# A fused feed-forward / attention / feed-forward block: picked rows corrected in DRAM, and one bias addition moved from GpSimd to VectorE

## The reference, cut to what matters

```python
x = x + 0.5 * ffn(layernorm(x), gate_w, gate_b, w1, w2)          # x: 8 x 1024 x 512
x = x + attn(layernorm(x), Wq, bq, Wk, bk, Wv, bv, Wo, bo)
x = x + 0.5 * ffn(layernorm(x), gate_w, gate_b, w1, w2)

def ffn(x):                                    # 32 experts, each picks 8 tokens of every batch
    probs = softmax(x @ gate_w.T + gate_b, axis=tokens)
    vals, idx = top_k(probs, 8)                # per batch and expert, over the 1024 tokens
    merged = sum_k vals * x[idx]               # one vector per batch and expert
    o = w2(gelu(w1(merged)))                   # both with a bias row, hidden size 2048
    return zeros.at[idx].add(vals * o)         # only picked tokens change

def attn(x):                                   # 16 heads of 32, linear attention
    q, k, v = exp(x Wq + bq), exp(x Wk + bk), x Wv + bv
    return (q . cumsum(k v^T)) / (q . cumsum(k)) @ Wo + bo
```

## Time and profile before

| | us |
|---|---|
| median of 3 runs (2296.61 to 2299.26) | 2297.79 |
| the profiled execution | 2299.73 |
| its span, first to last instruction | 2298.0 |
| TensorE busy | 1981.2 (86%) |
| TensorE weight loads busy | 1172.0 (51%) |
| ScalarE busy | 815.3 (35%) |
| VectorE busy | 734.2 (32%) |
| GpSimd busy | 647.2 (28%) |
| granted TensorE clock, mean | 0.937 |
| DMA | 762.76 MB, 332 GB/s over the span |

### The profile page before, as it was taken

The page is one execution under the profiler, slowest core; times in us unless marked ns, Lnnn a source line. Parts: engine busy times, 40 slices in busy tenths (PEclk is TensorE's granted clock), DMA queues, the critical chain, the costliest instruction groups (busy, mean ns, idle before and its releaser), DMA issues.

```text
span 2298.0 us, 44195 instructions
## 1 busy us (share of the span) xinstructions
PE 1981.2 (86%) x18664; PEld 1172.0 (51%) x18664; DVE 734.2 (32%) x1248; ACT 815.3 (35%) x1525; POOL 647.2 (28%) x783
## 2 busy tenths in 40 slices
PE   5789999999999999999999999999775666656666
PEld 3546666666666666676767767766521111111111
DVE  6731111111111111467677677677410000000011
ACT  6831121111111122477777777777510000000000
POOL 7620000000000000377777777777402000000002
PEclk9899999999999999999999999999987768887788
DMA  9999999999999999366554454444699999999997
GB/s 361 346 392 401 422 428 420 422 423 419 430 418 427 420 420 397 120 221 217 158 161 149 151 161 155 151 142 157 233 412 424 427 389 428 428 427 428 428 428 335
DMA packets 113844, 762.76 MB, mean 332 GB/s; under 512 B 21736, under 2 KB 21864, under 8 KB 76016
## 3 DMA queue, kind: packets, MB, share of 16 engines
q1 hardware_dynamic: 101552, 701.35, 76.9%
q10 hardware_dynamic: 9216, 50.34, 5.3%
q0 software_dynamic: 2880, 8.25, 0.9%
HBM read 648.65 MB, written 106.43 MB: 329 GB/s over the span
## 4 chain that ended last, share of the span: by engine, by line
PE 57%; DMA 23%; POOL 8%; ACT 5%; issue 4%; SPq 1%; DVE 1%; POOLq 0%; ACTq 0%; DVEq 0%
PE ps L316 53%; DMA big<-in_L_ffn_w 22%; PE ps L320 3%; POOL big L1475 2%; POOL s L1478 2%; DMA last_scratch<-idx 1%; SPq L18 1%; POOL big L1449 1%; ACT big L600 1%; POOL s L1460 1%; ACT big L1301 1%; POOL big L1480 1%; PE ps L787 1%; ACT big L585 1%; POOL big L1472 1%
## 5 line engine op out<-in xcount | busy, mean ns | idle before, releaser
L316 PE MATMUL ps<-big 128*32 128x512 f32 (+4 forms) x13792 | 985.2, 418 | 225.7 <-DMA big<-in_L_ffn_w 183.9
L316 PEld LDWEIGHTS ps<-big 128*32 128x32 f32 (+2 forms) x13792 | 385.9, 127 | 720.3 <-issue 383.4
L324 DVE TENSOR_TENSOR big<-ps,big 128x128 f32<-128x128 f32 (+3 forms) x375 | 343.7, 931 | 676.3 <-PE ps L787 509.6
L316 PE MATMUL ps<-wth,xth 128*128 128x512 f32 x768 | 311.8, 406 | 1.5 <-DVE xtl L324 1.5
L316 PE MATMUL ps<-wtl,xth 128*128 128x512 f32 x768 | 299.6, 390 | 0.0
L316 PE MATMUL ps<-wth,xtl 128*128 128x512 f32 x768 | 299.3, 390 | 0.0
L835 ACT COPY big<-ps 128x512 f32<-128x512 f32 x64 | 37.5, 586 | 650.8 <-PE ps L316 650.8
L1467 POOL TENSOR_SCALAR big<-big 128x1 f32<-128x1 f32 x64 | 12.3, 192 | 847.3 <-ACT ps L1279 844.8
L976 ACT ACTIVATE big<-ps,big 128x512 f32<-128x512 f32 x128 | 88.2, 689 | 371.8 <-PE ps L316 359.1
L985 DVE TENSOR_SCALAR big<-ps,big 128x512 f32<-128x512 f32 x64 | 48.0, 750 | 533.7 <-PE ps L316 533.7
L316 PE MATMUL ps<-wo,s 128*128 128x512 f32 x768 | 210.1, 409 | 3.4 <-ACT big L1349 1.9
(11 more groups left out here) (128 smaller groups left out, 1753.3 us busy)
## 6 DMA issues: line engine op xcount, KB each, us to landing
big<-in_L_ffn_w SPq DMA_DIRECT2D x254, 2048.0 KB, 18.0
p_scratch<-big ACTq DMA_DIRECT2D x64, 768.0 KB, 11.0
big<-p_scratch SPq DMA_DIRECT2D x64, 768.0 KB, 5.9
big<-in_L_attn_x SPq DMA_DIRECT2D x68, 256.0 KB, 3.0
xt_scratch<-big SPq DMA_DIRECT2D x16, 1024.0 KB, 8.2
big<-xt_scratch SPq DMA_DIRECT2D x16, 1024.0 KB, 15.8
x_weight_scratch<-big SPq DMA_DIRECT2D x64, 256.0 KB, 3.3
out_x<-big SPq DMA_DIRECT2D x64, 256.0 KB, 3.6
```

Of the source, the lines that this page charges most:

```text
L316: return nc.tensor.matmul(o, l, r, start=start, stop=stop, skip_group_check=True)
L324: return nc.vector.tensor_tensor(o, p, q, op)
```

## The change

From the third batch on (`TILED = 2`), tiles are no longer corrected one by one. Instead, q, k, v, x and the write-back weights of a batch lie side by side in DRAM (`rowd`, 2080 floats a token). The picked tokens' numbers are found with a rank and a top 8 on VectorE during experts 2 and 3 (`rows_dve`), laid out by SP in expert 6 (`rows_sp`). For each batch b from 2 to 7, POOL gathers 2 x 128 picked rows (iteration 8b - 12), TensorE transposes their weights (8b - 10) and makes their corrections (8b - 9 and 8b - 8), VectorE adds them, POOL scatters the rows back (8b - 7 and 8b - 6), and the tiles of the batch are then loaded already corrected. For those tiles VectorE does one sum over x (`tensor_reduce`) in place of the three correction operations. x and the write-back weights are copied into `rowd` by SP. The addition of the output bias to x1 (POOL's 1480) goes to VectorE at the end of its iteration, for all tiles. Four weight chunks of the second experts are loaded at other iterations. The square of ACT's line 1279 goes to SBUF instead of PSUM for tiles 16 to 51.

```diff
@@ turns, by iteration
+        TILED = 2
+        def turn(n, after):
+            b, k = divmod(n + 12 - after, 8)
+            return b if k == 0 and TILED <= b < B else None
@@ merging of the first gating: one buffer for each batch in place of two
-            act.wait_ge(s_mtok, e if e >= 8 else e - 1)
+            if e >= 8:
+                act.wait_ge(s_mtok, e)
@@ experts_sp, experts_dve
+                if p == 0 and e == 6:
+                    rows_sp(sp)
+                if p == 0 and 2 <= e < 4:
+                    rows_dve(dve, e - 2)
@@ attention_sp
             def load_x1(n):
-                sp.dma_start(X1[n % 4], xs[n]).then_inc(d_x1[n % 4], 16)
+                if n >= 8 * TILED:
+                    sp.wait_ge(d_s, 32 * (n // 8 - TILED + 1))
+                sp.dma_start(X1[n % 4], xs[n] if n < 8 * TILED else x1d[n]).then_inc(d_x1[n % 4], 16)
+
+            def copy_x(n):
+                sp.dma_start(x1d[n], xs[n]).then_inc(d_xc, 16)
+
+            def store_w(b):
+                sp.dma_start(wd[b], MTK[b]).then_inc(d_w, 16)
 
             def load_p(n):
                 sp.wait_ge(d_pst[n % 2], 16 * (n // 2 + 1))
+                if n >= 8 * TILED:
+                    sp.wait_ge(d_s, 32 * (n // 8 - TILED + 1))
@@
-                if n == NT - 2:
-                    sp.wait_ge(s_c, NT)
+                if n < 2:
+                    store_w(n + 4)
+                    copy_x(2 * n + 20)
+                    copy_x(2 * n + 21)
+                if n in (2, 3):
+                    store_w(n + 4)
+                if n >= 2 and n + 22 < NT:
+                    copy_x(n + 22)
+                if n == 16:
+                    sp.wait_ge(s_c, 8 * TILED)
+                    load_chunk(sp, 4 * E + 4)
+                if n == 52:
+                    sp.wait_ge(s_gc, GC0 + NGR)
+                    sp.wait_ge(s_x1sq, NT - 12)
                     load_chunk(sp, 4 * E + 3)
-                    load_chunk(sp, 4 * E + 4)
+                if n in (54, 58):
+                    sp.wait_ge(d_s, 16 * NGR)
+                    load_chunk(sp, 4 * E + (n - 50) // 4)
@@
-                m = n + 2
-                if 0 <= m < NT and m % 8 == 7 and m // 8 + 2 < B:
-                    sp.wait_ge(s_c, m + 1)
-                    load_m(m // 8 + 2)
-                if n in (2, 6, 10):
+                if n == 2:
@@ attention_pe
+            def rows_turn_pe(n):
+                if not (turn(n, 2) or turn(n, 3) or turn(n, 4)):
+                    return
+                pe.wait_ge(s_st, n + 1)
+                for s_ in (s_tk, s_tqv):
+                    pe.wait_ge(s_, min(n + 3, 8 * TILED))
+                pe.wait_ge(s_x1sq, min(n + 3, 8 * TILED))
+                if turn(n, 2):
+                    rows_weights_pe(pe, turn(n, 2))
+                for i in range(2):
+                    if turn(n, 3 + i):
+                        rows_pe(pe, turn(n, 3 + i), i)
@@ before S
+                    if turn(n - 1, 2):
+                        pe.wait_ge(s_gwt, GW0 + turn(n - 1, 2) - TILED + 1)
+                    for k in range(2):
+                        if turn(n - 1, 3 + k):
+                            pe.wait_ge(s_ga, GA0 + 2 * (turn(n - 1, 3 + k) - TILED) + k + 1)
@@ in the place of the correction
-                if m < NT:
+                if m < 8 * TILED:
...
+                else:
+                    rows_turn_pe(n)
@@ after the transposes of q
+                if 0 <= n < 8 * TILED - 2:
+                    rows_turn_pe(n)
@@ attention_dve
+                if m < 8 * TILED:
+                    dve.wait_ge(s_c, m + 1)
                     nc.vector.scalar_tensor_tensor(out=X1[m % 4], in0=ps[:, 7, :], scalar=0.5, in1=X1[m % 4],
                                                    op0=ALU.mult, op1=ALU.add,
                                                    accum_out=SX1[m % 2]).then_inc(s_x1, 1)
...
+                elif m < NT:
+                    nc.vector.tensor_reduce(SX1[m % 2], X1[m % 4], AX.X, ALU.add).then_inc(s_x1, 1)
+                if turn(n, 2):
+                    rows_weights_dve(dve, turn(n, 2))
+                for i in range(2):
+                    if turn(n, 3 + i):
+                        rows_add_dve(dve, turn(n, 3 + i), i)
+                m = n + 1
+                if 0 <= m < NT:
+                    dve.wait_ge(s_bo2, 1)
+                    dve.wait_ge(s_x1sq, m + 1)
+                    tt(X1[m % 4], X1[m % 4], BO, ALU.add).then_inc(s_x1b, 1)
@@ attention_pool
-                    pool.wait_ge(s_kl, m + 1)
-                    nc.gpsimd.tensor_tensor(X1[j], X1[j], BO, ALU.add).then_inc(s_x1b, 1)
+                if turn(n, 0):
+                    rows_gather_pool(pool, turn(n, 0))
+                for i in range(2):
+                    if turn(n, 5 + i):
+                        rows_scatter_pool(pool, turn(n, 5 + i), i)
@@ new functions
+        def rows_sp(sp):
+            sp.wait_ge(s_pos, PO0 + 8)
+            for h in range(2):
+                sp.dma_start(idxd[h], IDX1[:, 8 * h:8 * h + 8]).then_inc(d_row, 16)
+            sp.wait_ge(d_row, RW0 + 32)
+            sp.dma_start(IDXG.rearrange("r (b i) -> r b i", i=2),
+                         idxd.rearrange("h p j -> (h p j)").rearrange("(b r i) -> r b i", r=128, i=2)).then_inc(d_idx, 16)
+
+        def rows_gather_pool(pool, b):
...
+            for i in range(2):
+                nc.gpsimd.indirect_dma_start(
+                    out=G[i], out_offset=None, in_=rowd[b],
+                    in_offset=bass.IndirectOffsetOnAxis(ap=IDXG[:, 2 * b + i:2 * b + i + 1], axis=0),
+                    bounds_check=S - 1, oob_is_err=False).then_inc(d_g, 16)
+
+        def rows_scatter_pool(pool, b, i):
+            pool.wait_ge(s_ga, GA0 + 2 * (b - TILED) + 2)
+            pool.wait_ge(d_s, 32 * (b - TILED) + 16 * i)
+            nc.gpsimd.indirect_dma_start(
+                out=rowd[b], out_offset=bass.IndirectOffsetOnAxis(ap=IDXG[:, 2 * b + i:2 * b + i + 1], axis=0),
+                in_=G[i], in_offset=None,
+                bounds_check=S - 1, oob_is_err=False).then_inc(d_s, 16)
+
+        def rows_weights_pe(pe, b):
+            pe.wait_ge(d_g, 32 * (b - TILED + 1))
+            for i in range(2):
+                for u in range(4):
+                    t = mm(ps[32 * u:32 * u + 32, 4, 128 * i:128 * i + 128], G[i][:, 3 * D:3 * D + E], IDN, True, True)
+            t.then_inc(s_gwT, 1)
+
+        def rows_weights_dve(dve, b):
...
+            nc.vector.tensor_copy(at(os_at, 256), ps[:, 4, 0:256]).then_inc(s_gwt, 1)
+
+        def rows_pe(pe, b, i):
...
+            for u in range(4):
+                R_ = slice(32 * u, 32 * u + 32)
+                t = mm(ps[:, 4 + u, :], GWT[i][R_, :], OS[b][R_, :], True, True)
+            t.then_inc(s_gc, 1)
+
+        def rows_add_dve(dve, b, i):
+            dve.wait_ge(s_gc, GC0 + 2 * (b - TILED) + i + 1)
+            P3 = G[i][:, 0:3 * D].rearrange("p (u n) -> p u n", u=3)
+            X_ = G[i][:, 3 * D + E:XP]
+            tt(P3, ps[:, 4:7, :], P3, ALU.add)
+            nc.vector.scalar_tensor_tensor(out=X_, in0=ps[:, 7, :], scalar=0.5, in1=X_, op0=ALU.mult,
+                                           op1=ALU.add).then_inc(s_ga, 1)
```

More of the change, by code:

```diff
@@ L33, in macaron_block @@
     xtd = nc.dram_tensor("xt_scratch", (B * S // 512, 128, 4, 512), F).ap()
-    pd = nc.dram_tensor("p_scratch", (NT, 128, 3, D), F).ap()
+    XP = 4 * D + E
+    rowd = [nc.dram_tensor(f"p_weight_x_scratch{b}", (S, XP), F).ap() for b in range(B)]
+    prow = [rowd[n // 8][128 * (n % 8):128 * (n % 8) + 128] for n in range(NT)]
+    pd = [r[:, 0:3 * D].rearrange("p (u d) -> p u d", u=3) for r in prow]
+    wd = [r[:, 3 * D:3 * D + E].rearrange("(c p) e -> p c e", p=128) for r in rowd]
+    x1d = [r[:, 3 * D + E:XP] for r in prow]
+    idxd = nc.dram_tensor("row_scratch", (2, 128, 8), mybir.dt.uint32).ap()
     XW = D + E
@@ L139, in macaron_block @@
         assert s.at == 4 * SLOT
+        TILED = 2
+        G = [at(w_at + 2 * SLOT - 64 + XP * i, XP) for i in range(2)]
+        GWT = [at(os_at + 128 * i, 128) for i in range(2)]
+        MTK = [at(m_at + 2048 + 256 * b, 256).rearrange("p (c e) -> p c e", c=8) for b in range(8)]
+        RANK1, POS = at(b_at - 1024, 1024), at(os_at, 1024)
         n3 = Area(hid_at)
@@ L1156, in attention_pe @@
                     pe.wait_ge(s_st, n)
-                    for s_ in (s_x1sq, s_tk, s_tqv):
-                        pe.wait_ge(s_, min(n + 2, NT))
+                    pe.wait_ge(s_x1sq, min(n + 2, NT))
+                    for s_ in (s_tk, s_tqv):
+                        pe.wait_ge(s_, min(n + 2, 8 * TILED))
+                    if turn(n - 1, 2):
[3 more added lines that the diff above has]
+                            pe.wait_ge(s_ga, GA0 + 2 * (turn(n - 1, 3 + k) - TILED) + k + 1)
                     for g in range(4):
@@ L1302, in attention_act @@
                                          scale=RS[m % 2]).then_inc(s_qe, 1)
-                    act.wait_ge(s_tk, m + 1)
```

(23 more changed lines are left out.)

61 lines of the change are left out of this document (45 added, 16 removed).

## The result

The changed kernel takes 2304.24 us (median of 9 runs, 2299.92 to 2308.74), the kernel before 2297.79: a ratio of 1.0026, 95% interval 1.0016 to 1.0036. The profiled execution took 2305.76 us, its span is 2304.0 (before 2299.73 and 2298.0), at the same mean clock, 0.937. The forecast was 2302.

What follows compares the result with a forecast made beforehand. TensorE's work and an equally tight loop through POOL were taken to bound the attention. Batches from iteration 14 -3.5, early turn +6.8, iterations 0 to 13 +1.2 gave +4.5 us: 2302 us, range 2287 to 2315.

Steps and rivals of the forecast that it cites:

- What bounds, and where a gain arrives: Attention: TensorE's work and an equally tight loop through POOL bound it; savings there reach the end in full.
- U to S shrinks by 0.6, not 1.14: Plain tiles without corrections: TensorE's step falls from 7.2 to 6.6 us, then waits for VectorE's state addition.
- What the corrections free, the bias addition takes back: Tight loop of two tiles: VectorE's bias addition holds POOL 0.6 us a tile, cancelling the 0.6 won; loop stays 20.8 us.
- Late turns cost nothing beyond the two tiles' gain: Rows' matmuls, iterations 14 to 48: two tiles win nothing on TensorE, lose nothing on POOL; within the -3.5 us.
- The gathers' 0.9 us beyond GpSimd's wait: Two gathers exceed POOL's gap by 0.9 us in a tile TensorE bounds: 0, up to 5 us without that cover.
- Early turn: Batch 2's rows, iterations 6 to 8: TensorE waits for corrections' additions and S comes late, +6.8 us.
- Iterations 0 to 13: Still-corrected tiles: the bias addition mostly fits POOL's wait, but costs 0.6 us in iterations 0 and 3 of a batch, +1.2 us.
- Moving the addition away from GpSimd "gives 0 by itself": POOL's 1480, 1.28 us, stood where POOL waits for X2's square anyway, so its removal gives 0.
- SyncE in expert 6: SP waits for two small DMAs behind weight chunks, but TensorE has its next expert's weights: 0, at most 5 us once.
- that rival: Gathers land late: from 14.5 us on TensorE's weight transposes wait; with 17 us, 2317 us in all; chance 0.15.
- the first rival: The bias addition does not hold POOL: loop 10.1 us a tile, some 36 tiles win 0.3 us, 2288 us; chance 0.25.
- the addition on top of the top-8 weights: Step out of n % 8 = 3: top-8 weights already hold POOL's 1449, the bias addition comes on top, loses 0.6 us.

Runs made afterwards that it cites:

- noturn: The changed kernel without the picked rows' turn: no gathers, rows' matmuls, VectorE additions for them or scatters, tiles 16 to 63 loaded uncorrected; 2290.7 us, ratio 0.9957.
- nobias: The changed kernel without any addition of the output bias, so the result lacks it; 2301.5 us, ratio 1.0003.
- hold2: The changed kernel with VectorE's bias addition waiting until GpSimd has ended its power for x, and the top-8 operations ahead of it; 2298.2 us, ratio 0.9996.
- bias_pool: The changed kernel with the bias addition back on GpSimd, everything else as it is; 2310.9 us, ratio 1.0051.
- best: The changed kernel with the edits of hold2 and split, and SyncE's reload of row numbers moved behind expert 8; 2292.5 us, ratio 0.9965.
- hold: The changed kernel with VectorE's bias addition waiting until GpSimd has ended its power for x, the top-8 operations behind it; 2305.1 us, ratio 1.0028.
- split: The changed kernel with the first of a batch's two gathers issued one tile earlier, so they are not back to back; 2304.9 us, ratio 1.0020.
- state: The changed kernel with TensorE's matmuls for the next state put ahead of those for the current tile's values; 2316.3 us, ratio 1.0080.

## Why the prediction was right

The time was right to 2 us, and that is in part luck: two errors of some 7 us each cancelled. From 16 to 64 the forecast had -3.5 us with late turns at no cost. Without turns (noturn) that stretch is 11.0 us shorter than before, and the turns take 7.4 of it back, so -3.6 was measured. Of the single steps:

- **What bounds, and where a gain arrives**: held. The stream starts at 1663.50 (before 1655.69), 7.8 us later, and the end is 6.0 later; the 1.8 between them lie within what the last stage differs by from trace to trace.
- **U to S shrinks by 0.6, not 1.14**: held, 6.6 us, with the wait for the state addition that was named: 22.4 us in 31 places, 3.3 in 10 before.
- **"What the corrections free, the bias addition takes back"**: the step that fails, in size. Without turn and without the addition's price a batch takes 84.35 us (nobias, hold2), 2.8 less than before. The addition takes 0.9 of that, a third. The forecast gave 0.6 us a batch for both together; measured, 1.9 (85.25). Its lock was taken at 0.6 us a tile and is 0.28 in the mean, since GpSimd's operations start inside the addition, not with it, or are small, or go first and hold VectorE instead. The table below says in which steps the rest arose.
- **Late turns cost nothing beyond the two tiles' gain**: wrong the other way, 1.8 us each. The gathers' 0.9 us beyond GpSimd's wait, priced at 0 to 5 in all, are part of it: the cover named for them, a tile that TensorE bounds, did not hide them; the store of X2 behind the gathers was not thought of. Four turns take 7.1 us.
- **Early turn**: +6.8 forecast, +7.8 measured (7.6 against noturn), same waits.
- **Iterations 0 to 13**: +1.2 forecast for the addition. From 1 to 6 nothing was lost, and of the +0.9 from 9 to 16 noturn gives 0.7 back, so that is the turn's.
- **Moving the addition away from GpSimd "gives 0 by itself"**: wrong once the corrections are gone. On GpSimd the addition costs 1.5 to 1.7 us a batch (bias_pool against nobias), and bias_pool is 6.6 us slower than after. In the kernel before the move costs 0.9 us a batch and gains nothing.
- **SyncE in expert 6**: priced at 0, at most 5; it was 1.4 in this trace, and no median shows it. The cover named (TensorE has its next expert's weights) was not deep enough in any of the nine traces.
- **Rivals**: gathers landed in 8.9 us, below the 14.5 where that rival decided. GpSimd was held, so the first rival's mechanism is false as stated, though the freed loop it described is what hold2 and best show. Its price was too high as well: it had 2288 us for a kernel whose GpSimd isn't held, and hold2 takes 2298.2.

The steps from U to U of a batch without rows' matmuls (into n % 8; n from 50 to 57), us, from the starts of U in the two timelines:

| step into | before | after | difference | forecast |
|---|---|---|---|---|
| 2 | 10.46 | 10.15 | -0.31 | 0 |
| 3 | 11.38 | 11.05 | -0.33 | 0 |
| 4 | 11.11 | 11.47 | +0.36 | +0.6 |
| 5 | 11.04 | 10.45 | -0.59 | -0.6 |
| 6 | 11.89 | 11.30 | -0.59 | -0.6 |
| 7 | 10.16 | 10.12 | -0.04 | +0.4 |
| 0 | 10.47 | 10.16 | -0.31 | 0 |
| 1 | 10.62 | 10.41 | -0.21 | -0.4 |
| sum | 87.13 | 85.11 | -2.02 | -0.6, given as -3.5 for six |

The two steps that TensorE bounds came out to 0.01 us. The steps that the forecast left at nothing, because GpSimd's chain was to be as long as before, won 0.3 each, and the one behind the two gave nothing back. Such a step, U to U, in the kernel before and then in the changed one:

```profile
1494.23 0.50 PE L316 MATMUL ps<-s,tri 128*128 128x512 f32 x1
...
1504.69 0.49 PE L316 MATMUL ps<-s,tri 128*128 128x512 f32 x1 [0.37 <-POOL s L1478]
```

```profile
1505.38 0.50 PE L345 MATMUL ps<-s,tri 128*128 128x512 f32 x1
...
1515.53 0.50 PE L345 MATMUL ps<-s,tri 128*128 128x512 f32 x1 [0.64 <-POOL s L1572]
```

The step into 4 loses about as much without the addition (11.42 us in nobias), so the addition on top of the top-8 weights, which the forecast named for it, is not its cause.

## What to carry to other kernels

Work that leaves the longest engine shows only up to the next wait: price what is next in every kind of tile, then price the helper that the saving needs (here the turns: 15.6 us spent to save some 2.8 us a batch). When a forecast comes out, check its terms one by one: here two errors hid each other. An operation of VectorE with two SBUF inputs cost GpSimd nothing here when it was made to start while GpSimd waits, by a semaphore rather than by its place in the queue (hold2); look then at what stands behind it in that queue (hold, 7 us worse). A burst of indirect DMA is felt by whoever waits for a single-buffered store. Spreading it showed in the median only once the chain beside it was free (best against hold2, but not split against after). A change of order can win in most tiles and lose in the one that lacks a step, so time it tile by tile (state).

## What the runs showed of the hardware

Held operations come out longer in the trace in both directions, with no wait for the other engine shown ahead of them: VectorE's 32x1024 operation 2.13 us instead of 1.27, its 128x512 addition 1.47 instead of 0.68, GpSimd's 128x512 product 2.05 instead of 1.05, its 128x1 operation 1.11 instead of 0.27. The price is the overlap and not the whole length of the other operation: 0.31 us for a start 0.23 us into an addition of 0.68. Beside two gathers of 1 MB each, single loads took SyncE up to 5.95 us to issue instead of 0.32 (at most 0.75 without gathers and scatters), and a store of 256 KB landed after 10.4 us (4.6 in the median).
